# A fused Mamba, MoE and attention kernel: batch 0's states and its first expert pass in two halves of 256 tokens

## What is computed

```python
x = x + attn_a(layernorm(x))    # state-space layer
x = x + ffn(layernorm(x))       # 8 experts, F = 512, dense
x = x + attn_b(layernorm(x))    # 16 heads of 8, chunked local mask
x = x + ffn(layernorm(x))       # the same experts again
```

```python
delta = clip(softplus(dt_raw @ W_dt.T + b_dt), 1e-4, 1)
decay = clip(exp(-delta * a), 1e-4, 1)
drive = (1 - decay) * (b_term * xb)
state = decay * state + drive           # one step for each token
y     = sum(state * c_term) + D * x_t
```

## Time and profile before

| | us |
|---|---|
| median of 3 runs | 1492.82 |
| lowest and highest run | 1489.45, 1494.48 |
| the profiled execution | 1493.85 |
| its span, first to last instruction | 1492.1 |

### The profile page before, as it was taken

How to read it: one execution, slowest core, us unless ns; L and a number is a source line. 1 busy time by engine, 2 the same in 40 slices (tenths; PEclk the granted TensorE clock), 3 DMA queues, 4 the chain that set the end, 5 groups by cost and what they waited for, 6 DMA issues and landing times.

```text
span 1492.1 us, 31350 instructions
## 1 busy us (share of the span) xinstructions
PE 1427.2 (96%) x12756; PEld 1236.2 (83%) x12756; DVE 950.3 (64%) x2125; ACT 773.0 (52%) x1037; POOL 504.3 (34%) x446
## 2 busy tenths in 40 slices
PE   5798999999999999999999999999999999999998
PEld 3587878888788888888888888888888888888887
DVE  5655686665856667567675785658755565566543
ACT  6364738653466545645456574555644444355321
POOL 4351553433423443135410671136503320331000
PEclk9999999999999999999999999999999999999999
DMA  5120341004210420124002500062004200510000
GB/s 170 52 58 15 102 123 31 16 15 121 40 38 23 135 40 1 45 99 83 9 2 81 137 8 9 2 164 61 1 2 121 40 2 1 138 24 2 1 7 8
DMA packets 82876, 75.50 MB, mean 51 GB/s; under 512 B 5532, under 2 KB 60860, under 8 KB 82732
## 3 DMA queue, kind: packets, MB, share of 16 engines
q1 hardware_dynamic: 82732, 73.50, 18.8%
HBM read 60.65 MB, written 12.83 MB: 49 GB/s over the span
## 4 chain that ended last, share of the span: by engine, by line
PE 77%; DVE 10%; ACT 5%; issue 5%; POOL 4%; DMA 1%; DVEq 0%; SPq 0%; POOLq 0%; ACTq 0%
PE pd L1003 25%; PE pg L275 7%; PE pu L275 7%; PE pg L277 6%; PE pu L276 6%; PE pg L276 6%; PE pu L277 6%; PE att_ps L680 3%; DVE h L1096 2%; PE att_ps L702 2%; POOL arena L631 1%; PE att_ps L707 1%; DVE ffn_rows L298 1%; POOL arena L633 1%; DVE x L1084 1%
## 5 line engine op out<-in xcount | busy, mean ns | idle before, releaser
L1058 ACT ACTIVATE h<-pg 128x512 f32<-128x512 f32 x512 | 303.5, 597 | 658.3 <-PE pg L277 655.2
L1003 PEld LDWEIGHTS pd<-w_down,h 128*128 128x128 f32 x4096 | 512.2, 192 | 31.8 <-issue 2.7
L1003 PE MATMUL pd<-w_down,h 128*128 128x128 f32 x4096 | 525.0, 276 | 0.8 <-DVE x L1084 0.8
L1096 DVE TENSOR_TENSOR h<-h,pu 128x512 f32<-128x512 f32 x512 | 345.5, 679 | 215.4 <-PE pu L277 213.9
L275 PE MATMUL pg<-ffn_x_hi,w_gate_hi 128*128 128x512 f32 x512 | 244.5, 477 | 1.5 <-DVE ffn_x_lo L358 1.5
L275 PE MATMUL pu<-ffn_x_hi,w_up_hi 128*128 128x512 f32 x512 | 205.3, 401 | 13.4 <-DVE h L1096 13.2
L276 PE MATMUL pu<-ffn_x_lo,w_up_hi 128*128 128x512 f32 x512 | 203.3, 397 | 0.0
L276 PE MATMUL pg<-ffn_x_lo,w_gate_hi 128*128 128x512 f32 x512 | 203.3, 397 | 0.0
L277 PE MATMUL pg<-ffn_x_hi,w_gate_lo 128*128 128x512 f32 x512 | 203.0, 397 | 0.0
L277 PE MATMUL pu<-ffn_x_hi,w_up_lo 128*128 128x512 f32 x512 | 202.9, 396 | 0.0
L905 POOL TENSOR_TENSOR att_arena<-att_arena 128x512 f32<-128x512 f32 (+1 forms) x72 | 72.8, 1011 | 352.6 <-DVE att_arena L777 352.3
(11 more groups left out here) (192 smaller groups left out, 1540.2 us busy)
## 6 DMA issues: line engine op xcount, KB each, us to landing
arena<-bc_spread SPq DMA_DIRECT2D x56, 256.0 KB, 4.8
att_arena<-v_rows SPq DMA_DIRECT2D x64, 144.0 KB, 4.0
qk_rows<-qk_parts SPq DMA_DIRECT2D x32, 256.0 KB, 2.3
...
```

Of the source, the lines that this page charges most:

```text
L1003: last = nc.tensor.matmul(pd[:, t * P:(t + 1) * P], h_b[:, d % NH, t * P:(t + 1) * P], wd[:, d % NCH, :], start=d % CPE == 0 and t == 0, s ...
L1058: nc.scalar.activation(h_b[:, c % NH, :], pg[c % 2][:, :], ACT.Silu).then_inc(gate_done, 1)
L1096: nc.vector.tensor_tensor(h, h, pu[d % 2][:, :], ALU.mult).then_inc(h_done, 1)
```

## The change

Main 0 is cut in two halves of 256 tokens. `HEADS` now has 17 entries, two for main 0. In main 0 a chunk step handles two weight chunks of 128 columns for 256 tokens in place of one for 512: chunks 0 to 15 take all 32 weight chunks through tokens 0 to 255, chunks 16 to 31 through tokens 256 to 511. `pg`, `pu` and `h` keep their shape (two halves of 256 columns). Down products and `weigh` follow, two experts at a time.

Batch 0's states are cut likewise. The setup does tokens 0 to 255 of all groups, keeps each group's last state in `state_mid`, and makes y and the head for these. The second half's groups stand at slots 2.7, 4.7, 6.7 and 8.7, its y at 9.7 and its head at 11.5. B and C of the second half reach VectorE by DMA (`bc_mid`, through `spread_mid`). The second decay exponentials are done in setup.

The raw weights no longer go round a ring: 16 blocks have 16 places (`w_raw`: the eight slots of h, four in `k_room`, which shares its space with k3, three in `att_arena`, one in `staged`), and gate and up blocks alternate. SP waits for none of them. Chunk c (even, under 16) waits for c + 2 low parts, and the first down product for `w_down`. GpSimd's splits 8 to 15 are moved from setup to slots -2 to 1.

Batch 1's raw x is loaded once batch 0's transposes are done, and its norm and transposes stand in setup, at slots -25.2 to -22. Its other slots move a little (groups at 10.7, 13.7, 16.4, 19.1 in place of 9, 12, 15, 18).

```diff
-T_HEAD = [-4.5, 25] + [NCH * m - 8 for m in range(2, NM)]
+HEADS = [(0, 0, TT // 2), (0, TT // 2, TT)] + [(m, 0, TT) for m in range(1, NM)]
+HEAD_OF = {(m, a): n for n, (m, a, _) in enumerate(HEADS)}
+T_HEAD = [-4.5, 11.5, 24.6] + [NCH * m - 8 for m in range(2, NM)]
+T_MID = dict(k=(2.7, 4.7, 6.7, 8.7), y=9.7)
...
-        return dict(ln=1.5, win=3.5, dt=6, k=(9, 12, 15, 18), y=23.5)
+        return dict(st=-25.2, rows=-24.2, ln=-22, win=0.7, dt=7.7, k=(10.7, 13.7, 16.4, 19.1), y=23.1)
...
+        bc_mid = [[q3[:, k, i * L // 2:(i + 1) * L // 2].bitcast(F32) for k in range(KT)] for i in range(2)]
+        state_mid = sb("state_mid", [P, KT])
+        w_raw = [h_b[:, i, :] for i in range(NH)] + [k_room[:, g, LEFT:LEFT + L] for g in range(4)] + room[5:8] + [u_b[:, 3, :]]
...
+                    for cols, done in ((slice(0, L // 2), dec_first), (slice(L // 2, L), dec_exp)):
+                        if done is dec_exp:
+                            act.dma_start(bc_d[0][:, L // 2:L], bc_t[:, L // 2:L]).then_inc(mid_out, 16)
+                            nc.scalar.activation(dx_0, xb_0, ACT.Copy, scale=pk("d_skip")).then_inc(dx_done, 1)
+                            yield -21
+                        for k in range(KT):
+                            nc.scalar.activation(dec_0[k][:, cols], delta[:, cols], ACT.Exp, scale=neg_a[:, k:k + 1]).then_inc(done, 1)
...
+                                d, bt = dec_0[k][:, second], bt_0[k % 2][:, second]
+                                dve.wait_ge(dec_exp, k + 1)
+                                link(nc.vector.tensor_scalar(d, d, 1e-4, 1.0, ALU.max, ALU.min))
+                                if k >= 2:
+                                    dve.wait_ge(scan_done, k - 1)
+                                link(nc.vector.scalar_tensor_tensor(bt, d, 1.0, xb_0[:, second], ALU.subtract, ALU.mult))
+                                link(nc.vector.tensor_tensor(bt, bt, bc_mid[0][k], ALU.mult))
+                                nc.vector.tensor_tensor_scan(d, d, bt, state_mid[:, k:k + 1], ALU.mult,
+                                                             ALU.add).then_inc(scan_done, 1)
+                                dve.wait_ge(scan_done, k + 1)
+                                nc.vector.tensor_tensor(d, d, bc_mid[1][k], ALU.mult).then_inc(y_done, 1)
...
-                        split3(pg[c % 2][:, :], [w[:, c % NCH, :] for w in wg],
-                               (fxh[m % 2][:, :], fxl[m % 2][:, :])).then_inc(g_full, 1)
+                        product(pg[c % 2], wg, c).then_inc(g_full, 1)
...
+                def product(out, w, c):
...
+                    a = f // (NCH // 2) * (L // 2)
+                    for j in range(2):
+                        last = split3(out[:, j * L // 2:(j + 1) * L // 2], [v[:, 2 * (f % (NCH // 2)) + j, :] for v in w],
+                                      [v[:, a:a + L // 2] for v in x])
+                    return last
...
-                        if j >= NH:
-                            sp.wait_ge(w_lo, j - NH + 1)
-                        sp.dma_start(h_b[:, j % NH, :], (wg_d, wu_d)[j // E][j % E]).then_inc(w_loaded[j % NH], 16)
+                        sp.dma_start(w_raw[j], (wg_d, wu_d)[j % 2][j // 2]).then_inc(w_loaded[j], 16)
...
-                        j = c + SETUP - 8
-                        if 0 <= j < 2 * E:
-                            split_w(j)
-                        return
+                    if c < 0 and 0 <= c + SETUP - 8 < E:
+                        split_w(c + SETUP - 8)
+
+                    if -2 <= c < 2:
+                        for j in range(2):
+                            split_w(E + 2 * (c + 2) + j)
```

320 lines of the change are left out of this document (199 added, 121 removed).

## The result

The changed kernel takes **1485.82 us** (median of 11 runs, 1483.10 to 1488.86); the kernel before, run beside it, 1492.82 us (11 runs, 1488.67 to 1494.86). The ratio is 0.9956, with a 95% interval of 0.9945 to 0.9966: 7.0 us or 0.5% faster, where 4.2 us were forecast. The profiled execution took 1486.64 us, span 1484.8 us, against 1493.85 and 1492.1.

A forecast was written before the change was run, and what follows sets the result against it. TensorE, busy 96% of the span, bounds the kernel, except in setup, where the chain runs through VectorE. Setup -12.0 and main 0 +7.8 give -4.2 us: 1488.6 us from the median 1492.82, range 1481 to 1495.

The forecast's parts named there:

- its own list of signs: Closing checks: wrong if passes stand at 0.15 us, first chunk after 46 us, or main 0 under 92 or over 100.
- VectorE's groups: Setup: four first-half state groups of 256 columns, 2.4 us each, about 8.0 us overlapped, ending at 35.6 instead of 46.4 us.
- The y product as the gate: Setup: TensorE's first-half y, not VectorE, comes last; bank free at 32.8 us, 24 passes take 5.7, done at 38.5.
- The head: Setup, from residual add to first chunk: 4.7 us for two tiles instead of 6.6 for four; first chunk at 43.2 us.
- 256-column passes: Main 0: 384 passes of 256 columns replace 192 of 512, at 0.127 us each; +4.0 us, bounds -0.2 to +14.8.
- The rival with every load by itself: Main 0: weight load and stream run one after the other, 0.223 us a pass, total 1526 us; chance 0.02.
- VectorE's chains: Main 0: four second-half state chains of 2.3 us between h products make TensorE wait; +2.0 us, bounds 0 to 5.
- Batch 1's groups and GpSimd: Main 0: groups 2.7 chunks (6.4 us) apart, GpSimd needs 8.15, VectorE waits with h products behind; +1.0 us (0 to 3).
- Table loads: Main 0: ScalarE loads its table twice more for the second head's exponentials; +0.5 us (0 to 3).
- Given back: Main 0: shorter VectorE wait for batch 2's x, and batch 1's norm out of the first chunks; -1.3 us (-3 to 0).
- moved passes: Main 0, TensorE: second-half y and head passes add 3.4 us, batch 1's transposes leave (0.7); +2.7 us.
- the loop absorbs it: Rival, main 0: new passes and VectorE chains fit beside existing waits, only 4 us come back; 1484.8 us, chance 0.22.

The follow-up runs named there:

- short chains: Changed kernel without the products with x and B and the scan in main 0's second-half state groups; 1488.24 us, ratio 0.9976 to the kernel before.
- later y: Changed kernel with GpSimd's splits 8 to 15 waiting for the head's row operations, plus batch 1's y at 23.6 instead of 23.1; 1487.92 us, ratio 0.9964.
- second profile of the changed kernel: The changed kernel, unchanged, run again in a second session beside the kernel before; 1486.33 us, ratio 0.9953.

## Why the prediction was right, and where it was not

The direction and the range were right, and so was the account of the setup but for its last step, the head; the size of main 0 was not, and 2.8 us of the total with it. By its own list of signs the prediction came close to being wrong: main 0 took 92.6 us, and under 92 was one of them.

**VectorE's groups**: 2.4 us each, 8.0 us in all; measured 7.9 (27.18 to 35.07), scan 0.69, products 0.42, copy 0.15. Right, term by term.

**The y product as the gate**: right. The bank was free at 31.5 in place of 32.8 us, since ScalarE began its exponentials at 26.64, half a microsecond earlier than assumed, and did four of them in 1.6, the four casts in 2.1 us, so that its copy started at 30.94; the 24 passes took 5.8 (forecast 5.7), and the addition began at 37.38, 1.1 us early.

**The head**: forecast 4.7 us, measured 43.92 - 37.38 = 6.5. Two steps of it failed. GpSimd's power has a length after all: 0.71 us for two columns, 1.03 for four. And the rows, at 0.28 each, were costed without asking what GpSimd does at that moment, though the prediction itself used this effect for the scans and its trace had the sizes. They took 1.9 us more. The splits moved out of the states' way stood in the rows' way. First chunk 11.3 us earlier instead of 12.0: two errors of opposite sign.

**256-column passes**: the term that failed, and at least as large as the whole difference in main 0 (3.2 us); the other misses largely cancel (below). It took columns and overhead apart, 0.107 + 0.02 a pass, and charged +4.0 us; the passes stand 0.118 us apart, next to the lower bound (0.116), which makes 384 x 0.118 - 44.7 = +0.6 at most. The 0.02 us of a 512 are no fixed price for a pass: at 256 columns 0.011 is left beside 0.107, half as much for half the columns. So the two rows had to be read as proportional, with the 128-column row as the one that pays for its load. The rival with every load by itself is excluded: load and columns one after the other, 0.116 and 0.107, would put the passes 0.223 us apart, and they stand 0.118 apart. That rival is what a rule of the Trainium skill would make of it (TensorE: Matmul & The Clock Gate, section "The mechanism"), by which a weight load overlaps a running matmul only when their row groups differ. The trace disagrees, with 0.118 us for passes that all use all rows.

**VectorE's chains**, +2.0 forecast: `pu`'s waits grew by 1.9. Right in size and place: h(0) and h(2) start 7.05 us apart (48.95 and 56.00), 7 were forecast, and the wait of 1.32 us is that of pu(4). The chain makes 1.3 of it, which is what the short chains took away; the other 0.5 is the convolution and the routing sums. **Batch 1's groups and GpSimd**, +1.0: 1.5 at one wait, TensorE's own for y, as the first of several that can take it (later y only passed it on). The forecast had it at the h products behind the groups, and there nothing was added: 1.8 us before and after. Its 6.4 us for 2.7 chunks have no row, either; at 2.25 us a chunk it is 6.1, at main 0's 88.0 us for 32 it is 7.4. **Table loads**, +0.5: no wait of TensorE is due to them.

**Given back**, -1.3 by a shorter wait for batch 2's x: not so. The wait is 4.67 us in place of 3.92:

```profile
115.13 0.87 DVE L306 BATCH_NORM_STATS2 bn_ssm_ln<-arena 128x6 f32<-128x128 f32 x4 [4.67 <-DMA arena<-in_x]
```

What was given back came from a source that the sum did not have. TensorE's first passes run at half pace, and the doubling came 4.7 us behind the first chunk (256s 0.21 us apart up to 48.5) in place of 7.0 (512s 0.43 apart up to 62.2): about 1.2 us, half of the difference. This is luck and no gain of the change: in the second profile of the changed kernel the doubling came after 6.9 us.

**Main 0 by the ledger.** Busy: counted from start to start at full clock, with the turns from bank to bank, a 512 costs 0.258 us before and a 256 0.128 after, so the gate and up passes make -0.4; with 2.7 for moved passes, as forecast, and -1.2 for the pace it is 1.1 against 1.3 measured. Idle: 1.9 + 1.5 = 3.4 against 3.35. The forecast had 6.7 busy and 1.1 idle, after its gifts. Against it, the passes are 4.4 less, the pace 1.2, the tables 0.5 and the h waits 0.1; the y wait is 0.5 more, and what was to be given back (1.3) or absorbed in gaps (1.1) was not. (The 83.7 us busy that it set beside main 0's 88.0 belong to a window of 89; within main 0 it is 82.96.) Its rival "the loop absorbs it" gave the better total (1484.8), but for another reason than its own: TensorE did not hide passes in idle time, its idle time grew.

**The total**: the runs moved by 7.0, chunk 32 by 6.7. That the two agree is in part chance, since the pace at the start gives chunk 32 about 1.2 us in these two profiles.
